# First attention of a fused block: mixing in rounded halves, token-major scores, pooling transposed at once, gate weights folded into the values, the batch loop unrolled

## The reference

```python
Q_char = _linear(char_emb, Wq_c, bq_c)            # char_emb: layernorm(x), (4, 1024, 256)
K_sub = _linear(subword_emb, Wk_s, bk_s)          # subword_emb: context, (4, 77, 256)
V_sub = _linear(subword_emb, Wv_s, bv_s)
char2sub = softmax(Q_char @ K_sub.T * scale) @ V_sub
Q_sub = _linear(subword_emb, Wq_s, bq_s)
K_char = _linear(char_emb, Wk_c, bk_c)
V_char = _linear(char_emb, Wv_c, bv_c)
sub2char = softmax(Q_sub @ K_char.T * scale) @ V_char     # (4, 77, 256)
sub2char = _interp_linear(sub2char, 1024)                 # 77 rows -> 1024 rows
gate = sigmoid(concat([char2sub, sub2char]) @ Wg.T + bg)
x = x + tanh(g_xattn[0]) * (gate * char2sub + (1 - gate) * sub2char)
```

## Time and profile before

| | |
|---|---|
| time, median of 3 runs | 1170.46 us (1170.24 to 1170.55) |
| span of the profiled execution | 1171.8 us |
| PE busy | 1107.9 us (95%) |
| PEld busy | 854.4 us (73%) |
| DVE busy | 547.1 us (47%) |
| ACT busy | 434.8 us (37%) |
| POOL busy | 94.6 us (8%) |
| chain that ended last | PE 84%, DVE 7%, ACT 4% of the span |
| of it L773 (the MLP's products) | 54% |
| of it L615, L616, L618 (the mixing) | 4% |

### The profile page before, as it was taken

One profiled execution on the slowest core, in us unless ns is written; L12 is line 12 of the kernel. 1 busy time (PEld: TensorE's weight loads), 2 busy tenths in 40 slices (PEclk: granted clock), 3 DMA queues, 4 the chain that ended last, 5 costly groups with the idle time before them and its releaser, 6 DMA issues.

```text
span 1171.8 us, 15039 instructions
## 1 busy us (share of the span) xinstructions
PE 1107.9 (95%) x5066; PEld 854.4 (73%) x5066; DVE 547.1 (47%) x1500; ACT 434.8 (37%) x812; POOL 94.6 (8%) x130
## 2 busy tenths in 40 slices
PE   6988888989999999899999999999999999999997
PEld 4655555757767677678888888888888888788886
DVE  4657566767767677651241341431421512412411
ACT  0233342112424226263353353343443533533532
POOL 0121121110000000120000100100100100000000
PEclk8999998999999999899999999999999999999999
DMA  9100000061000000300000000000000000000000
GB/s 356 62 1 1 0 0 1 1 287 37 1 36 0 1 36 1 144 1 1 1 18 1 18 0 0 18 0 0 18 0 0 18 0 0 18 0 0 19 1 20
DMA packets 5172, 32.69 MB, mean 28 GB/s; under 512 B 1166, under 2 KB 1422, under 8 KB 3080
## 3 DMA queue, kind: packets, MB, share of 16 engines
q1 hardware_dynamic: 4584, 29.41, 6.3%
q10 hardware_dynamic: 544, 2.75, 0.7%
HBM read 27.97 MB, written 4.19 MB: 27 GB/s over the span
## 4 chain that ended last, share of the span: by engine, by line
PE 84%; DVE 7%; ACT 4%; issue 3%; DMA 1%; DVEq 1%; SPq 0%; POOL 0%; POOLq 0%; ACTq 0%
PE psum L773 54%; PE psum L670 12%; PE psum L689 2%; PE psum L467 2%; PE psum L615 2%; DVE x_residual L1342 2%; PE psum L521 1%; PE psum L538 1%; PE psum L697 1%; PE psum L545 1%; PE psum L650 1%; PE psum L717 1%; PE psum L616 1%; PE psum L618 1%; DMA mlp_out_scale<-in_w_s 1%
## 5 line engine op out<-in xcount | busy, mean ns | idle before, releaser
L773 PE MATMUL psum<-hidden_a_high,mlp_rest_rounded 128*128 128x512 f32 x512 | 199.7, 390 | 0.0
L773 PE MATMUL psum<-hidden_a_low,mlp_rest_rounded 128*128 128x512 f32 x512 | 199.3, 389 | 0.0
L773 PE MATMUL psum<-hidden_b_high,mlp_h_rounded 128*128 128x512 f32 x512 | 199.2, 389 | 0.0
L773 PE MATMUL psum<-hidden_b_low,mlp_h_rounded 128*128 128x512 f32 x512 | 199.2, 389 | 0.0
L1454 DVE TENSOR_TENSOR hidden_a_low<-hidden_a,hidden_a_high 128x512 fp32r<-128x512 f32 x128 | 88.3, 690 | 195.4 <-ACT hidden_a_high L1049 194.5
L1342 DVE SCALAR_TENSOR_TENSOR x_residual<-psum,expert_weight,x_residual 128x256 f32<-128x256 f32 (+1 forms) x256 | 108.4, 477 | 56.5 <-PE psum L670 55.7
L1454 DVE TENSOR_TENSOR hidden_b_low<-hidden_b,hidden_b_high 128x512 fp32r<-128x512 f32 x64 | 44.3, 693 | 180.1 <-ACT hidden_b_high L1049 178.7
L670 PE MATMUL psum<-expert_high,x_T_high 128*128 128x512 f32 x256 | 113.2, 442 | 3.1 <-DVE x_residual L1342 3.1
L773 PEld LDWEIGHTS psum<-hidden_a_high,mlp_rest_rounded 128*128 128x128 f32 x512 | 96.1, 188 | 21.4 <-DVE hidden_a_low L1454 1.5
L773 PEld LDWEIGHTS psum<-hidden_b_low,mlp_h_rounded 128*128 128x128 f32 x512 | 96.1, 188 | 19.9
L773 PEld LDWEIGHTS psum<-hidden_b_high,mlp_h_rounded 128*128 128x128 f32 x512 | 96.1, 188 | 19.9
(11 more groups left out here) (195 smaller groups left out, 1562.1 us busy)
## 6 DMA issues: line engine op xcount, KB each, us to landing
x_residual<-in_x SPq DMA_DIRECT2D x4, 1024.0 KB, 22.1
mlp_h_slice<-in_h SPq DMA_DIRECT2D x4, 1024.0 KB, 4.6
mlp_rest<-in_h SPq DMA_DIRECT2D x1, 4096.0 KB, 19.8
mlp_h<-in_h SPq DMA_DIRECT2D x1, 4096.0 KB, 12.2
out<-x_residual SPq DMA_DIRECT2D x8, 512.0 KB, 2.7
mlp_rest<-in_w SPq DMA_DIRECT2D x3, 1024.0 KB, 8.8
expert_in<-in_Wi SPq DMA_DIRECT2D x1, 2048.0 KB, 15.4
expert_out<-in_Wo SPq DMA_DIRECT2D x1, 2048.0 KB, 19.8
```

The costliest lines, as they stand in the source:

```text
L773: last = mm(o, a, b, start=(k == 0 and i == 0), stop=(k == n_k - 1 and i == len(parts) - 1))
```

## The change

- The mixing uses rounded operands. The probabilities, the values and the pooled rows are each split into a high half (rounded, by ACT) and a low half (the rest, by DVE). A tile is now seven products instead of three: high x high, high x low and low x high for the values, and the rounded interpolation matrix with the high and the low half of the pooled rows, twice.
- The scores are computed token-major at once: the transposed tile is stationary, the map moves, and the bias is added by a product of a row of ones with a row of biases.
- The pooling is computed transposed, so its own transpose goes. Its scaling by the softmax sum is moved behind the product.
- The gate's weights are multiplied into the value weights once (`Wv_c`, loaded in addition, times `WgT1`), and the bias likewise; the gate's share of the pooled rows then comes from the same rows as their values.
- The loop over batches is written out; copies of the batch's maps go. `TILE_BEFORE` and `EXPERTS_AFTER` follow the shorter list of steps.

The core of the diff:

```diff
-EXPERTS_AFTER = {0: (0, 1), 1: (2, 3), 2: (4, 5), 3: (6,), 4: (7,)}
-TILE_BEFORE = (0, 1, 4, 5, 6, 8, 8, 9)
+EXPERTS_AFTER = {0: (0, 1), 1: (2, 3), 2: (4, 5), 3: (6, 7)}
+TILE_BEFORE = (0, 1, 4, 5, 5, 6, 6, 7)
...
             pe.wait_ge(val_v, 2 * B)
+            pe.wait_ge(map_v, 4)
+            for m in range(KC):
+                for k in range(KC):
+                    mm(ps[:, 0, m * D:(m + 1) * D], wa("Wv_c")[:, k, m * P:(m + 1) * P], wa("WgT1")[:, k, :],
+                       start=(k == 0), stop=(k == KC - 1))
+            for k in range(KC):
+                last = mm(ps[0:L, 1, 0:D], col("bv_c", k).broadcast_to([P, L]), wa("WgT1")[:, k, :],
+                          start=(k == 0), stop=(k == KC - 1))
+            last.then_inc(fw_ps, 1)
...
             def a_scores(c):
-                pe.wait_ge(s1_s, 2 * c + 2)
-                for j in range(JT):
-                    last = pe.transpose(ps[:, 4 + j // G, (j % G) * L:(j % G + 1) * L],
-                                        s1s[:, j * P:(j + 1) * P], ident[0:L, 0:L])
+                bias = c1row[:, c * L:(c + 1) * L].unsqueeze(1).broadcast_to([1, G, L])
+                for q in range(2):
+                    mm(ps[:, 4 + q, 0:G * L].rearrange("p (j c) -> p j c", j=G), oner[:], bias, start=True, stop=False)
+                    for i in range(G):
+                        j = q * G + i
+                        for k in range(KC):
+                            last = mm(ps[:, 4 + q, i * L:(i + 1) * L], xnT[:, k, j * P:(j + 1) * P],
+                                      A1[:, k, c * L:(c + 1) * L], start=False, stop=(i == G - 1 and k == KC - 1))
+                    last.then_inc(s1b_ps, 1)
...
             def a_sum(b, j):
                 if j == 0:
+                    pe.wait_ge(vh_r, B)
+                    pe.wait_ge(vl_r, B)
                     pe.wait_ge(p1t_v, 2 * b + 2)
-                    pe.wait_ge(so_v, b + 1)
-                    pe.wait_ge(sg_v, b + 1)
+                    pe.wait_ge(p1l_v, 2 * b + 2)
+                    pe.wait_ge(sh_r, b + 1)
+                    pe.wait_ge(sl_r, b + 1)
...
-                mm(ps[:, first, :], P1T[:, t], of(VV, b), start=True, stop=False)
...
+                mm(ps[:, first, :], P1Th[:, t], VVh[:, b, :], start=True, stop=False)
+                mm(ps[:, first, :], P1Th[:, t], VVl[:, b, :], start=False, stop=False)
+                mm(ps[:, first, :], P1Tl[:, t], VVh[:, b, :], start=False, stop=False)
+                mm(ps[:, first, D:2 * D], IT[:, t], SSh[:, b % 2, D:2 * D], start=False, stop=False)
+                mm(ps[:, first, D:2 * D], IT[:, t], SSl[:, b % 2, D:2 * D], start=False, stop=True)
+                mm(ps[:, second, 0:D], IT[:, t], SSh[:, b % 2, 0:D], start=True, stop=False)
+                mm(ps[:, second, 0:D], IT[:, t], SSl[:, b % 2, 0:D], start=False, stop=True).then_inc(fin, 1)
...
-            with pe.Fori(1, B) as c:
+            for c in range(1, B):
...
+            def a_sub2char(c):
+                act.wait_ge(sf_v, 2 * c + 2)
+                if c >= 2:
+                    act.wait_ge(fin, (c - 1) * JT)
+                act.activation(SSh[0:L, c % 2, :], SSf[0:L, :], ACT.Copy).then_inc(sh_r, 1)
...
+            def values_low(b):
+                dve.wait_ge(vh_r, b + 1)
+                dve.tensor_tensor(VVl[0:L, b, :], vf[:, b % 2, :], VVh[0:L, b, :].bitcast(F32), ALU.subtract
+                                  ).then_inc(vl_r, 1)
             for b in range(B):
                 dve.wait_ge(val_ps, b + 1)
+                if b == 2:
+                    dve.memset(VVl[64:LP].bitcast(F32), 0.0).then_inc(zero_ready, 1)
+                    dve.wait_ge(zero_ready, 3)
+                    values_low(0)
+                    values_low(1)
+                    dve.wait_ge(vl_r, 2)
...
+            dve.wait_ge(fw_ps, 1)
+            dve.tensor_copy(wa("Wv_c"), ps[:, 0, :].rearrange("p (k c) -> p k c", k=KC)).then_inc(fw_v, 1)
+            dve.tensor_copy(bvg[:], ps[0:L, 1, 0:D]).then_inc(fw_v, 1)
...
+            def a_sub2char_low(c):
+                dve.wait_ge(sh_r, c + 1)
+                dve.tensor_tensor(SSl[0:L, c % 2, :], SSf[0:L, :], SSh[0:L, c % 2, :].bitcast(F32), ALU.subtract
+                                  ).then_inc(sl_r, 1)
```

233 lines of the change are left out of this document (109 added, 124 removed).

## The result

| | before | after |
|---|---|---|
| median of the timed runs | 1170.51 us (4 runs, 1170.24 to 1172.32) | 1187.22 us (4 runs, 1181.51 to 1191.89) |
| ratio | | 1.0137, 95% interval 1.0106 to 1.0167 |
| span of the profiled execution | 1171.8 us | 1190.0 us (run time 1191.89) |
| first transposes / tile 0 of the first batch | 38.70 / 76.13 us | 48.38 / 90.73 us |
| passes, from tile 0 to tile 0 | 37.1 us each | 36.52 and 45.99 us |

The change made the kernel 16.7 us slower. Forecast were 6.6 us more, and a range that ended at 1182.5. The four runs of the kernel before lie within some 2 us here, those of the changed one within 10, so part of the answer is what differs between executions of one program.

A forecast was written before the change was run, and what follows sets the result against it. The prediction took PE to bound the passes, losing time to waits for DVE and ACT. It summed 6.3 + 1.6 + 1.5 - 0.5 + 0.5 - 2.8 = +6.6 us to 1177.1 us, range 1166 to 1182.5.

The forecast's parts named there:

- setup with the fold: Before the first transposes: longer chain and inputs cost 6.3 us, the folded weight at half clock 1.5 us more.
- first batch: From the first batch's scores to its tile 0, 18.9 us before: 1.6 us more, at full clock.
- passes: Three passes: 36.9 us each instead of 37.1, full clock back 6.5 us after tile 0; 0.5 us gained in all.
- exit: Behind the last pass: the longer gap puts more work under half clock, 0.5 us more.
- last batch's tiles: In the first expert pass: five tiles gain 0.57 us each, 2.8 us less.
- walk of a pass: PE, DVE and ACT followed from tile 0: 34.4 us a pass before clock effects, PE idle 6 us at its end.
- clock stays low through both turns: Rival for the passes: full clock only 12 us after tile 0, 38.6 us a pass, 1182.1 us in all; chance 0.12.
- 3 us were enough: Argument from the earlier trace's setup: PE stopped at 15.5 us and the clock fell at about 18.5.
- the clock holds: Rival: no clock fall in the passes, 8.1 us gained there, fold at full speed, 1167.5 us in all; chance 0.18.

The follow-up runs named there:

- c2: The changed kernel with filler products in the gaps before the first tile 0 and behind each pass: 1177.21 us, ratio 1.0036.
- e2: The changed kernel with filler in every gap, including the 1.26 us before the first batch's pooling: 1177.37 us, ratio 1.0061.
- f2: The changed kernel with the scores' bias held in 128 rows instead of one and filler in every gap: 1170.52 us, ratio 0.9978.
- c1: The changed kernel run again with nothing edited, for a second trace: 1195.11 us, ratio 1.0204.
- c4: The changed kernel with the fold run earlier, one zeroing moved to POOL and low halves of values before the saves: 1185.12 us, ratio 1.0120.
- d1: The kernel before, with six unread DVE subtractions delaying tile 0 of each batch, 4.3 us expected: 1196.67 us, ratio 1.0210.
- d3: The changed kernel with d2's reordered end of a pass and one tile before each of the eight steps: 1179.77 us, ratio 1.0082.
- d2: The changed kernel with transposed probabilities ahead of sub2char's high half on ACT, low halves ahead of tile 7's update on DVE: 1182.30 us, ratio 1.0074.
- f1: The changed kernel with only the scores' bias held in 128 rows instead of one, gaps left unfilled: 1179.97 us, ratio 1.0057.
- c3: The changed kernel with scores and pooling back in wide products of 512 and 256 columns: 1198.45 us, ratio 1.0213.
- e3: c3 with its one-row bias products replaced by 128-row ones, the scores' bias left out: 1185.73 us, ratio 1.0118.

## Why the prediction was wrong, point by point

The first trace, in the terms of the sum:

| term | forecast | measured | how |
|---|---|---|---|
| setup with the fold | +7.8 | +9.68 | 48.38 - 38.70 |
| first batch | +1.6 | +4.92 | (90.73 - 48.38) - (76.13 - 38.70) |
| passes | -0.5 | +9.18 | (211.50 - 90.73) - (187.72 - 76.13) |
| exit | +0.5 | +0.46 | transposes to first expert product, 7.69 - 7.23 |
| last batch's tiles | -2.8 | -2.7 | start to end of the stretch in which they lie |
| one stall on DVE | none | -2.7 | see below |

- *The walk of a pass was right, the account of the clock was not.* PE became the one that waits, for the low half of sub2char; the gap before tile 0 was forecast at 6 us and is 5.96 in the first pass. The walk gave 34.4 us for a pass at full clock; c2 and e2 have 35.6, f2 34.84 and 34.81. A tile was put at 1.15 us: in the third pass two successive tiles start 1.26 us apart, and the products behind them 1.16 us later. The exit and the last batch came out within 0.1 us.
- *The step that failed is the clock's, the term "-0.5 (passes)" and the full speed taken for the first batch.* The sum lets the clock fall only in the gap before a tile 0 and has it back 6.5 us behind it, for "36.9 a pass". In the first trace the first pass did so (back after 4.0 us, 36.52 us) and the third nearly (6.9 us; 38.26 us with the exit, 37.31 before). The second had full speed back after 5.1 us, lost it again at 142.6 us while PE was busy, and took 45.99: that is 8.9 of the 9.2 us in the row "passes". The first batch lost it too, which is most of the 3.3 us above its term.
- *When the clock comes back.* Over the nine passes of the first trace, c1 and c4, full speed was back 4.0 to 6.9 us behind tile 0 five times and 11.7 to 13.3 us four times. The 6.5 us were about right for five, but one assumed value stood for both. The passes without another fall took 36.5 (back after 4.0), 38.0 (6.9) and 39.0 us (11.7), where the prediction had 35.9, 36.9 and 38.6 for 4.4, 6.5 and 12. The rival "clock stays low through both turns" (38.6 us a pass) had the size of c1 and c4, and its 0.12 was too little; it did not have what happened in the first trace. The Trainium skill's rule on it (TensorE: Matmul & The Clock Gate, Part 4), that transposes do not count as activity, would make the turns run at half; four of the nine passes agree.
- *What no rival had: half clock that begins while PE is busy.* I looked for falls in gaps only. The second pass lost it behind a one-row product and stayed at half for 24 us, some 9 us of time. I had priced those bias products by columns alone, at 0.26 us an instruction (they take 0.36), and never asked how much of the array they use. The Trainium skill (TensorE: Matmul & The Clock Gate, Part 1) says that the gate follows how busy PE has been. The gaps agree (d1); the one-row products don't, since PE was busy 6.00 of 6 us before the fall and 23.00 of 23 at 0.50.
- *The first batch.* The clock fell at 77.7 us, 1.5 us behind a wait of 1.26 us, where I had written "the wait for the last expert's low half and the copy to 9.9; pooling to 13.3", all at full speed. Scores to tile 0 took 25.23 us, of which scores 5.20 and, mostly at half clock, the pooling 5.75, L590 3.67 and the transposes 1.91. The wait is needed but not enough: the fall came in the first trace, c1, c2, c4 and d3 and is gone with the wait filled (e2), but it also stayed away with the wait in place in d2 and f1, and in the kernel before, c3 and e3, whose pooling has wide products. One-row products earlier in the batch, the narrow products of the pooling and the moment at which the wait falls are all left as reasons.
- *Setup.* The inputs cost 1.0 instead of 0.45 us, and the fold ran entirely at half clock, 5.5 us instead of 4.1. The chain itself was as described, and c4 shows its worth, 11 us to the first transposes. My reading of the earlier trace rows was half a microsecond early: a clock of 0.76 over 18 to 20 us puts the fall at 19.0, not 18.5, and 0.57 over 25 to 26 us puts the return at 25.9, not 25.4. So "3 us were enough" was 3.5.
- *The rival "the clock holds"* was worked out at 1167.5; f2, which is the change with full clock in the passes, takes 1170.5. With both causes removed 16.7 us of the first median come back (1187.22 to 1170.52, in two sessions whose medians of the kernel before are 1170.51 and 1172.80), though f2 still has the slow setup. Some 2.6 us of it are not the clock's but the shorter bias products and scores, 0.64 us in each of four batches (an estimate from the rows of e2 and f2). The rest, the larger part of the loss, is the clock in the first attention.
- *The stall.* DVE in the profiled execution of the kernel before stood still for 2.64 us at 381 us, without a releaser, and PE behind it for 1.79. The first trace of the changed kernel and d1's have no such wait there. It flatters the first trace by 2.7 us and is not explained. With it the rows of the table come to 18.8 us; the spans differ by 18.2, and the rest is spread in steps of 0.1 to 0.2 us over the expert passes.

What stays open: why equal passes of one program (the two of c1, or the first and second of the first trace) differ; what the first batch's fall needs besides the wait; and whether narrow products or those with the identity add to the falls behind the bias products, since only the one-row products were exchanged. f1 left 8 us of spread and f2 6, with its twelve runs between a clock of 0.985 at 1173 us and 0.992 at 1167 us; where in the program that difference lies no trace here tells.
